# Attention slots of four heads by 256 queries in place of two heads by 512, and a first transfer cut in five pieces

## What is computed

```python
qh, kh, vh = heads(x @ Wq), heads(latent_kv @ W_up_k), heads(latent_kv @ W_up_v)   # (4, 16, 1024, 8)
scores = jnp.einsum('bhqd,bhkd->bhqk', qh, kh) * scale
decay = jnp.exp(-LAMBDA_DECAY * TIME_STEP * jnp.abs(idx[:, None] - idx[None, :]))
attn = jax.nn.softmax(clip(scores) * decay, axis=-1)
out = jnp.einsum('bhqk,bhkd->bhqd', attn, vh) ... @ Wo
```

## Time and profile before

| | us |
|---|---|
| median of 3 runs | 540.0 (538.99 to 542.82) |
| the profiled execution | 537.49 |
| its span, first to last instruction | 535.6 |
| TensorE busy in the span | 491.2 (92%) |
| ScalarE busy | 487.1 (91%) |
| VectorE busy | 279.4 (52%) |
| GpSimd busy | 218.1 (41%) |

### The profile page before, as it was taken

How to read it: one execution, slowest core, us unless ns; L and a number is a source line. 1 busy time by engine, 2 the same in 40 slices (tenths; PEclk the granted TensorE clock), 3 DMA queues, 4 the chain that set the end, 5 groups by cost and what they waited for, 6 DMA issues and landing times.

```text
span 535.6 us, 9389 instructions
## 1 busy us (share of the span) xinstructions
PE 491.2 (92%) x3457; PEld 113.3 (21%) x3457; DVE 279.4 (52%) x652; ACT 487.1 (91%) x528; POOL 218.1 (41%) x281
## 2 busy tenths in 40 slices
PE   8767999999999999999999999999999999999951
PEld 3311211231121211231121212222111212121210
DVE  5523454454744555554754554554555655455546
ACT  2756999999999999999999999999999999999941
POOL 0789406974251218993251217994101211002110
PEclk9998999999999999999999999999999999999995
DMA  5368979746997101757977100747987000100000
GB/s 174 121 229 210 278 220 242 274 143 201 261 206 182 48 5 33 278 170 213 256 164 161 26 5 7 276 170 223 259 181 165 22 5 7 47 0 1 1 21 24
DMA packets 48707, 73.79 MB, mean 138 GB/s; under 512 B 6096, under 2 KB 26512, under 8 KB 48528
## 3 DMA queue, kind: packets, MB, share of 16 engines
q1 hardware_dynamic: 47840, 72.85, 49.3%
q10 hardware_dynamic: 816, 0.28, 0.2%
HBM read 35.40 MB, written 35.65 MB: 133 GB/s over the span
## 4 chain that ended last, share of the span: by engine, by line
PE 47%; ACT 32%; issue 9%; DVE 5%; DMA 3%; POOL 2%; SPq 1%; DVEq 0%; POOLq 0%; ACTq 0%
ACT probs L730 32%; PE ps L926 25%; PE ps L910 14%; PE ps L828 1%; PE ps L795 1%; PE ps L823 1%; PE ps L791 1%; DVE ps L1150 1%; PE ps L800 1%; DMA qp_dram<-parts 1%; DMA Qs<-qp_dram 1%; DMA X<-L_attn_x 1%; PE ps L835 0%; POOL parts L589 0%; POOL sq L587 0%
## 5 line engine op out<-in xcount | busy, mean ns | idle before, releaser
L730 ACT ACTIVATE probs<-ps 128x1024 f32<-128x1024 f32 x512 | 479.8, 1065 | 17.3 <-DVE ps L1150 11.6
L926 PE MATMUL ps<-probs,V 128*9 128x512 f32 x2048 | 268.6, 596 | 3.9 <-DVE pv_out L1158 1.2
L1150 DVE TENSOR_TENSOR ps<-ps,consts 128x256 f32<-128x256 f32 (+1 forms) x256 | 144.4, 566 | 182.6 <-PE ps L910 175.9
L910 PE MATMUL ps<-Qs,Ks 64*128 64x512 bf16 x992 | 181.8, 386 | 18.1 <-ACT probs L730 5.1
L910 PEld LDWEIGHTS ps<-Qs,Ks 64*128 64x128 bf16 x992 | 43.8, 93 | 289.5 <-ACT probs L730 267.7
L926 PEld LDWEIGHTS ps<-probs,V 128*9 128x9 f32 x2048 | 31.3, 88 | 79.3 <-issue 58.3
L626 POOL TENSOR_TENSOR xs<-xs,magic 128x512 f32<-128x512 f32 x7 | 8.9, 1277 | 92.4 <-DVE magic L1211 92.4
L543 POOL TENSOR_SCALAR rs<-mv 128x4 f32<-128x4 f32 (+1 forms) x10 | 2.3, 228 | 82.7 <-DVEq L1332 82.0
L565 POOL TENSOR_TENSOR sq<-kT,decay 128x256 f32<-128x256 f32 (+2 forms) x13 | 16.2, 1249 | 47.8 <-DVE kT L1250 33.4
L1158 DVE COPY pv_out<-ps 105x512 f32<-105x512 f32 x31 | 21.4, 692 | 25.8 <-PE ps L926 25.8
L577 POOL TENSOR_TENSOR sq<-sq,parts 128x1024 f32<-128x1024 f32 (+1 forms) x16 | 29.3, 1834 | 1.3
(11 more groups left out here) (142 smaller groups left out, 285.7 us busy)
## 6 DMA issues: line engine op xcount, KB each, us to landing
Qs<-qp_dram SPq DMA_DIRECT2D x26, 512.0 KB, 9.5
qp_dram<-parts SPq DMA_DIRECT2D x16, 768.0 KB, 4.7
Ks<-kp_dram SPq DMA_DIRECT2D x26, 384.0 KB, 5.9
kp_dram<-parts SPq DMA_DIRECT2D x12, 384.0 KB, 3.8
kp_dram<-parts SPq DMA_DIRECT2D x6, 768.0 KB, 5.0
qp_dram<-parts SPq DMA_DIRECT2D x8, 512.0 KB, 6.0
Qs<-qp_dram SPq DMA_DIRECT2D x12, 256.0 KB, 8.5
X<-L_attn_x SPq DMA_DIRECT2D x10, 256.0 KB, 3.0
```

The costliest lines, as they stand in the source:

```text
L730: nc.scalar.activation(probs[:, quad % RING, 2 * jp:2 * jp + 2, :].rearrange("p j n -> p (j n)"), ps_all[:, bank * CH:(bank + 2) * CH], AC ...
L910: last = nc.tensor.matmul(bank, Ks[half, g, jp, key_cols(v, kc)], Qs[half, g, jp, qh, v, :], start=True, stop=True)
L926: last = nc.tensor.matmul(pv[32 * j:32 * j + VW, :], V[:, unit // 2 * NB + kc, HG * j + g, :], probs[:, quad % RING, j, :], start=i == 0, ...
L1150: nc.vector.tensor_tensor(own, own, factors, ALU.mult).then_inc(fixed, 1)
```

## The change

Behind group 0 a slot becomes four heads by 256 queries. A group's 16 slots are the eight key blocks for its first 256 queries, then for the other 256 (`h` is the half). `qk(s)` issues four bf16 matmuls of 256 columns, `weigh` is called for every slot, with four float32 matmuls of 256 columns each, three slots behind `qk`. Because a half's queries meet only two diagonal key blocks, 4 of 16 slots have a fix, each of 4 x 128 elements; with group 0 there are 132 fixes, where there were 256. The ring of `probs` is six slots, where it was four quads. The exponential itself stays at 128x1024.

The keys are held as 14 signed blocks of 128 columns, where there were 12 (KN is 1792, it was 1536). The early parts of the first sequence come in five pieces: keys, first half of the queries, keys, second half of the queries, the last two key blocks. TensorE waits for `stage_in[1]` before quad 8, `stage_more` before quad 10, `stage_last` before quad 12.

```diff
-KP = S - 2 * P
-KN = 2 * KP
+KN = KL + S + 2 * P
...
-FIRST_PIECES = ("early keys 0", "early queries", "early keys 1", "late keys", "late queries")
+FIRST_PIECES = ("early keys 0", "early queries 0", "early keys 1", "early queries 1", "early keys 2", "late keys",
+                "late queries")
...
-    if r < 2:
-        return PLUS, (0, (r + 1) * P, (1 - r) * P)
-    return MINUS, (r * P, CH, 2 * P)
...
+    unit, _, h, kc = place_of(s)
+    r = kc - 2 * (2 * (unit % 2) + h)
+    if r < 0 or r > 1:
         return (PLUS if r < 0 else MINUS), None
+    return (PLUS, (0, P, P)) if r == 0 else (MINUS, (P, 2 * P, 2 * P))
...
             pool.wait_ge(k_sb, 1)
-            decayed_keys(PLUS, slice(0, 2 * P), 0)
-            decayed_keys(MINUS, slice(2 * P, CH), 2 * P)
+            decayed_keys(PLUS, slice(0, P), 0)
+            decayed_keys(MINUS, slice(P, CH), P)
             split(0, CH, 0)
             pool.wait_ge(q0_ready, 2)
-            split_queries_of_first_group()
+            split_queries_of_first_group(0)
             pool.wait_ge(k_sb, 2)
             decayed_keys(MINUS, slice(CH, S), 0)
             split(0, CH, CH)
+            split_queries_of_first_group(1)
+            decayed_keys(PLUS, slice(P, 3 * P), 0)
+            split(0, 2 * P, S)
+            normalise(1)
             late_keys(0)
-            normalise(1)
             late_queries(0)
...
             def qk(s):
...
-                for i in range(2):
-                    bank = ps[:, 2 * (s % 3) + i, :]
...
+                for t in range(2):
+                    for i in range(2):
                         half = slice(64 * i, 64 * i + 64)
-                        last = nc.tensor.matmul(bank, Ks[half, g, jp, key_cols(v, kc)],
-                                                Qs[half, g, jp, qh, v, :], start=True, stop=True)
+                        last = nc.tensor.matmul(ps[:, 2 * (s % 3) + i, t * HQ:(t + 1) * HQ],
+                                                Ks[half, g, t, key_cols(v, kc)],
+                                                Qs[half, g, t, qh, h, v * HQ:(v + 1) * HQ], start=True, stop=True)
                 last.then_inc(qk_done, 1)
...
+            def weigh(s):
...
+                for j in range(HG):
+                    at = (j % 2 * 2 + j // 2) * HQ
+                    last = nc.tensor.matmul(pv[32 * j:32 * j + VW, h * HQ:(h + 1) * HQ],
+                                            V[:, unit // 2 * NB + kc, HG * j + g, :], probs[:, s % RING, at:at + HQ],
+                                            start=i == 0, stop=i == NB - 1)
                 last.then_inc(pv_done, 1)
...
+            def weigh_after(s):
...
+                elif at == 4:
+                    weigh(s - 4)
+                    weigh(s - 3)
+                elif at != 3:
+                    weigh(s - 3)
...
+                    for s in (2 * quad, 2 * quad + 1):
                         pe.wait_ge(exp_done, s - 2)
+                        qk(s)
+                        weigh_after(s)
```

More of the change, by code:

```diff
@@ L66, in pieces_out @@
 def pieces_out(b, which):
-    return 2 * b + (1 if which == 0 and b > 0 else 0)
+    return 2 * b + (2 - which if b > 0 else 0)
 RSQRT_MAGIC = float(0x5F3759DF)
@@ L568, in decayed_queries @@
                 cols = slice(qh * CH, (qh + 1) * CH)
-                q2 = qT[:, cols].rearrange("p (o n) -> p o n", o=1).broadcast_to([P, 2, CH])
-                chain(nc.gpsimd.tensor_tensor(rest.rearrange("p (v n) -> p v n", v=2), q2, decay[:, :, cols], ALU.mult))
+                for h in range(2):
+                    own = slice(cols.start + h * HQ, cols.start + (h + 1) * HQ)
+                    q2 = qT[:, own].rearrange("p (o n) -> p o n", o=1).broadcast_to([P, 2, HQ])
+                    chain(nc.gpsimd.tensor_tensor(rest[:, h * CH:(h + 1) * CH].rearrange("p (v n) -> p v n", v=2), q2,
+                                                  decay[:, :, own], ALU.mult))
             def split(which, n, at):
                 r = rest[:, 0:n]
-                to = [parts[:, which, k, at:at + n] for k in range(PARTS)]
+                to = [parts[which][:, k, at:at + n] for k in range(PARTS)]
                 chain(nc.gpsimd.tensor_copy(to[0], r))
@@ L721, in _ @@
             for s in range(SLOTS):
[L722 to L725 removed]
+                if s >= RING:
+                    act.wait_ge(pv_done, s - RING + 1)
+                if variant(s)[1] is None:
                     act.wait_ge(qk_done, s + 1)
@@ L920, in weigh @@
                     pe.wait_ge(k_sb, 2)
-                elif i == 0:
-                    pe.wait_ge(pv_copied, quad // NB)
+                pe.wait_ge(v_sb, 1 + quad // 4)
+                for j in range(HG):
+                    jp, i = divmod(j, 2)
+                    last = nc.tensor.matmul(pv[32 * j:32 * j + VW, :], V[:, quad, HG * j, :],
+                                            probs[:, (2 * quad + jp) % RING, i * CH:(i + 1) * CH],
+                                            start=quad == 0, stop=quad == NB - 1)
+                last.then_inc(pv_done, 2)
+            def weigh(s):
+                unit, g, h, kc = place_of(s)
+                i = s % NB
+                pe.wait_ge(exp_done, s + 1)
+                if s % GROUP_SLOTS == 0:
+                    pe.wait_ge(pv_copied, s // GROUP_SLOTS)
                 if g == 0:
@@ L965, in _ @@
                     second_keys()
-            weigh(QUADS - 2)
-            weigh(QUADS - 1)
+            for s in range(SLOTS - 3, SLOTS):
+                weigh(s)
             pairs = (range(0, 2), range(2, 4))
@@ L1140, in fix @@
             def fix(s):
-                quad = s // 2
-                _, span = variant(quad)
+                _, span = variant(s)
                 if span is None:
@@ L1380, in _ @@
             for half in range(2):
[L1381 removed]
+                dve.wait_ge(pv_done, SLOTS)
                 if half == 0:
```

196 lines of the change are left out of this document (114 added, 82 removed).

## The result

The changed kernel takes 560.54 us (median of 4 runs, 559.11 to 561.36), the kernel before in the same comparison 539.62: a ratio of 1.0386, 95% interval 1.0355 to 1.0416. It is slower, by 3.9%, and lies 3.5 us above the 557.0 predicted. The profiled execution took 560.11 for a span of 558.3 us.

The account below looks back on a forecast made before the run. TensorE was taken to bound groups with jobs, ScalarE those without. Slot 32 at 54.0, plus 478 for groups 2 to 31, plus the 21.96 tail less 0.4, gave a 553.5 us span, so 557 median; range 546 to 568.

Parts of the forecast that it names:

- The slot: TensorE's scores and values per slot: 0.88 us, or 1.76 a quad where it was 1.51.
- The fixed part: TensorE's change from scores to values and back: 0.25 us for the two, now paid every slot, not every quad.
- The rival without the fixed part: TensorE's fixed part does not come twice: slot 0.76 to 0.80, total 521 to 530 us; chance 0.07.
- Weight loads: Rival: second score pair's 92 ns load on TensorE no longer hidden; slot 0.97, total 598 us; chance 0.04.
- The group sums: Groups 2 to 31: 14.3 us each plus jobs, 478 in place of 454.2, 24 us more; group 13 near 17.5.
- The start: Groups 0 and 1: slot 16 at 37.6, 4.8 us earlier; slot 32 at 54.0, 5.4 us less.
- Transfers in the stream: Key stores and loads a sixth larger, DMA share 0.5 over the stream: taken as 0, at worst 2 us.
- The fixes: VectorE's fixes fall from 256 to 132: worth at most 11.6 us, nothing where TensorE sets the pace.
- The signs to look for: Among them: ScalarE waiting for scores, not fixes; mean exponential falling from 1065 ns towards 1.02 us; group 13 near 17.5.

Follow-up runs that it names:

- pairs run: Changed kernel with values weighed for two slots together behind every second slot of scores; 548.94 us, ratio 1.0177.
- after_wholeq: Changed kernel with both halves of the first queries split and stored before the second keys; 562.73 us, ratio 1.0434.
- before_gather8: Kernel before with first queries in two pieces, first unit's next-stream key stores behind group 3's gather, every unit's reciprocal one quad later; 535.08 us, ratio 0.9925.
- pairs_best: Changed kernel with paired values, late queries stored earlier, diagonal blocks third and seventh, unit 0's reciprocal one quad later; 545.78 us, ratio 1.0108.
- before_gather: Kernel before with first queries in two pieces and, in the first unit, next-stream key stores behind group 3's gather; 537.04 us, ratio 0.9951.
- before_pipe: Kernel before with only the first queries split in two halves, each stored and loaded by itself; 537.74 us, ratio 0.9978.
- pairs_qstore: Changed kernel with paired values and the first sequence's late query stores ahead of the second gather; 545.66 us, ratio 1.0112.

## Why the prediction was right

- **The slot** was the term that decides, 0.88 us, and measured 0.87 to 0.88. The fixed part stayed whole: scores to values 0.32 = 0.21 + 0.11, values to scores 0.55 = 0.42 + 0.13. The pairs run shows it as the cause: one return for two slots takes 1.08 us off group 13. The rival without the fixed part fell by it. On this the Trainium skill, page TensorEngine Tiling (Array Packing), Key Properties (a change of tiling mode drains the engine), and the trace agree; scores and values differ in type too (bf16, float32), and no run holds the two apart.
- **Weight loads** under 256 columns stayed hidden, and the 0.97 and 598 us of that rival fell too. By what the Trainium skill, page TensorE: Matmul & The Clock Gate, states under "What overlaps and what doesn't" (a load overlaps a running matmul only where the row groups differ), they would have shown; the trace does not agree, as the second pair of scores is on the rows of the first and adds its columns alone.
- **The group sums**: group 13 predicted near 17.5, measured 17.44; 478 us for groups 2 to 31, measured 480.6 (56.03 to 536.58). But two errors cancel within. Group 5's late gather costs 4.35 us that the sum did not hold, and the other groups came out 1.8 us below it.
- **The start**: slot 16 at 37.6 predicted, 38.82 measured, and 37.8 in the runs where the first exponential began near 16.3. After, it began at 17.41, with a stretch at half clock from 12.4 to 15.8 us in the projections. Five of the fourteen profiled executions show such a stretch (first exponentials at 17.3 to 17.7, in the others at 15.9 to 16.4), kernels with the old slot and with the new among them, so it is owed to no edit here. Slot 32 was predicted at 54.0 and came at 56.03: these 1.2, and 0.8 mostly since the waits for keys in group 1 were 1.8 and 0.7 us, 2.5 together where I took 1.5. The reason given was wrong in part. I had the gain from a store that begins 2.9 us earlier and carries half, and the load as long as before (0.6 + 4.65). `after_wholeq` stores both halves first, all but 0.6 us as late as the kernel before, and slot 16 comes as early: there a load of half the queries (2.9 us from its last issue) and key loads issued ahead of it make up for 3.3 us.
- **Transfers in the stream**: "nothing waits for it there, I take 0, at worst 2" is the step that failed. The average DMA share of 0.5 hid 0.75 to 0.80 over groups 2 to 9, and "nothing waits" was not so even before: the reciprocal's waits of 0.45 and 1.39 us showed that its gathers landed just in time or late. It was in the trace, and I did not look for it. The span missed by 4.8 us (558.3 against 553.5): 4.35 for this, 2.0 for the start and 0.1 for the tail, less the 1.8 above; the rest is rounding. That the time falls so near the forecast, and inside the range, is in part luck: 4.35 us that were put at nothing stand against 1.8 us of a sum that was too long.
- **The fixes**: worth nothing where TensorE paces, which the runs confirm in group 13 (17.44 with and without). In group 14, without jobs, they cost 0.74 us after, and 2.5 over groups 10 to 31.
- **The signs to look for** were poor in two cases. ScalarE's waits are put down to fixes (27.6 of 37.7 us), not to scores, although without fixes the idle time is the same. And the mean exponential fell only to 1051 ns; in the run without fixes it is 1102. Neither tells what paces the kernel; the stretch of a group and TensorE's starts do.
- Not settled: the 4.3 us by which groups 10 to 31 of the kernel with pairs stay above the kernel before (336.48 against 332.19), 0.2 us a group. The second kernel with pairs (fixes moved) showed only that they can't be had by the place of the fixes.

## What to carry to other kernels

Split each step of a kernel into a part by columns and a part paid at each change of kind of matmul, start to start; then a smaller slot is priced by how many more changes it makes. When two kinds alternate, let two slots share one change, whatever the slot's own size. Before you count an early lead as gained, look for the transfers that land just in time now: here waits of 0.45 and 1.39 us were all that told of the 5 us that the lead gave back. When a repair of one transfer moves the wait to the next unit, try the consumer too: it helped once (`before_gather8`), where it moved by more than the wait, and not in `pairs_best`. And before a profile is read as an edit's effect, see that the row that changed lies behind the edit.

## What was unexpected of the hardware

- A TensorE wait can cost more than itself. After 3.27 us of idling its clock was at half for 3.4 us (granted 0.50 from 111.4 to 114.8), which by my estimate costs about 1.7 us of work on top (half of the 3.4). It does not always come: in `after_wholeq` a wait of 2.76 us at 91.61 was followed by such a stretch, and one of 2.77 us at 43.27 was not. The Trainium skill, page TensorE: Matmul & The Clock Gate, tells of half clock behind waits for transfers under "HAM oscillation — how this bites in real kernels"; the trace agrees for the wait in group 5.
- One VectorE instruction (`wide<-rec,consts`, 128x512 float32) runs 98 times in the fourteen profiles. In the 53 places in which GpSimd did nothing it took 0.69 us, whatever the DMA share (0.69 at 99.89 us in `before_gather` with a share of 1.05). Where a GpSimd instruction was already running when it began, it ended 0.54 to 0.55 us after that one's end, or after its own 0.69 if that was later: 1.42 after (107.89, GpSimd's subtraction ended 0.87 in), 1.53 in `before_pipe`, 1.59 and twice 1.03 in `before_gather8`, up to 1.74 in `pairs_qstore`. It held for subtractions, products and casts alike. A GpSimd instruction that began behind it cost it nothing. So it looks as if the one waits for the other to end, rather than both going slower. The Trainium skill, page GPSIMD Engine Reference, section Key points, says that the two engines share their SBUF interfaces and contend when VectorE reads two SBUF inputs, as this instruction does; the trace agrees.
- The same order of instructions gave two starts, 15.9 to 16.4 or 17.3 to 17.7 us for the first exponential, by whether TensorE's clock was at half for 3.4 us in the projections (after from 12.4 to 15.8; in the other four it began at 12.0 to 13.0). A difference of 1.4 us between two single profiles of a kernel with such a start says nothing.
